# Last stage of a graph kernel: one-hots made on ScalarE, eight of seventeen row tiles split into float32r heads and tails

## What is computed

```python
def _L1_gnn_ref(feat, src_idx, dst_idx, in_deg, W1, b1, W2, b2):
    agg = jax.ops.segment_sum(feat[src_idx], dst_idx, num_segments=num_dst)
    ah = agg / in_deg[:, None]
    return jnp.einsum('nf,of->no', feat[:num_dst], W1) + b1 + jnp.einsum('nf,of->no', ah, W2) + b2

h = jnp.maximum(_layernorm(x, axis=-1), 0.0)
x = x + _L1_gnn_ref(h, src, dst, deg, W1, b1, W2, b2)
```

## Time and profile before

| | before |
|---|---|
| median of 3 runs | 1931.77 us |
| the profiled execution | 1932.3 us |
| its span (first to last instruction) | 1930.5 us |
| the last stage's row tiles on PE (L929), first to last | 1338.8 to 1915.9 us |
| mean granted clock of PE | 0.949 |
| busy over the span: PE, DVE, ACT, POOL | 86%, 69%, 52%, 59% |

### The profile page before, as it was taken

One profiled execution on the slowest core, in us unless ns is written; L12 is line 12 of the kernel. 1 busy time (PEld: TensorE's weight loads), 2 busy tenths in 40 slices (PEclk: granted clock), 3 DMA queues, 4 the chain that ended last, 5 costly groups with the idle time before them and its releaser, 6 DMA issues.

```text
span 1930.5 us, 24219 instructions
## 1 busy us (share of the span) xinstructions
PE 1666.8 (86%) x5735; PEld 963.8 (50%) x5735; DVE 1336.3 (69%) x2587; ACT 1001.1 (52%) x3779; POOL 1141.1 (59%) x1323
## 2 busy tenths in 40 slices
PE   3799863688988889898888897895999999999998
PEld 1344331466666666666666666342444444444443
DVE  8768994888888989898988885465444444444441
ACT  4453313499999999999999997241000000000000
POOL 2000001878787878888787880013777777777773
PEclk9899876799999989999999999997999999999999
DMA  8122104665657565665657562945777777777774
GB/s 188 52 69 71 63 28 145 192 168 143 192 150 190 160 184 170 168 186 163 191 149 197 145 179 61 222 109 153 210 217 212 219 218 219 216 214 211 215 213 140
DMA packets 133201, 318.07 MB, mean 165 GB/s; under 512 B 41908, under 2 KB 42158, under 8 KB 133044
## 3 DMA queue, kind: packets, MB, share of 16 engines
q0 software_dynamic: 70240, 229.93, 41.8%
q1 hardware_dynamic: 62804, 86.44, 16.2%
HBM read 280.43 MB, written 35.86 MB: 164 GB/s over the span
## 4 chain that ended last, share of the span: by engine, by line
PE 51%; DVE 20%; issue 15%; POOL 7%; DMA 4%; ACT 2%; DVEq 1%; SPq 0%; POOLq 0%; ACTq 0%
PE wide L769 14%; PE sums L929 12%; PE sums L832 12%; PE wide L860 9%; POOL arena L504 7%; DVE nodes L1338 2%; DVE arena L1083 2%; DVE arena L1082 2%; DMA h2tab<-node 2%; DVE nodes L1284 1%; DVE nodes L1329 1%; DVE node L1225 1%; PE wide L782 1%; PE wide L787 1%; ACT arena L582 1%
## 5 line engine op out<-in xcount | busy, mean ns | idle before, releaser
L636 ACT ACTIVATE nodes<-arena,nodes 128x64 f32<-128x64 f32 x2840 | 682.7, 332 | 1.2 <-PE sums L832 1.2
L504 POOL DMA_INDIRECT arena<-ktab,idx x425 | 421.5, 992 | 188.1 <-issue 142.2
L504 POOL DMA_INDIRECT arena<-h2tab,idx x425 | 445.7, 1049 | 135.8 <-issue 134.9
L832 PE MATMUL sums<-nodes,oh 128*125 128x260 f32 x1768 | 466.7, 407 | 47.0 <-DVE nodes L1284 47.0
L769 PE MATMUL wide<-w_sb,node 128*125 128x512 f32 x1000 | 465.6, 610 | 20.7 <-ACT node L567 12.3
L832 PEld LDWEIGHTS sums<-nodes,oh 128*125 128x125 f32 x1768 | 342.0, 198 | 123.3 <-DVE nodes L1284 58.4
L929 PE MATMUL sums<-arena,oh 128*125 128x512 f32 x850 | 375.9, 600 | 6.9 <-DMA arena<-h2tab,idx 6.5
L716 ACT ACTIVATE node<-wide 128x500 f32<-128x500 f32 x51 | 27.3, 585 | 570.9 <-PE wide L915 570.8
L860 PE MATMUL wide<-q_win,node 125*128 125x512 bf16 x1275 | 310.3, 381 | 3.0 <-issue 3.0
L769 PEld LDWEIGHTS wide<-w_sb,node 128*125 128x125 f32 x1000 | 187.0, 193 | 230.8 <-issue 201.8
L1329 DVE TENSOR_TENSOR nodes<-wide,arena 128x1024 f32<-128x1024 f32 (+1 forms) x225 | 258.6, 1159 | 12.4 <-PE wide L860 11.8
(11 more groups left out here) (202 smaller groups left out, 1165.9 us busy)
## 6 DMA issues: line engine op xcount, KB each, us to landing
node<-node_tab SPq DMA_DIRECT2D x27, 531.2 KB
q_win<-qtab SPq DMA_DIRECT2D x26, 336.0 KB
arena<-ktab,idx POOLq DMA_INDIRECT x425, 5.1
arena<-h2tab,idx POOLq DMA_INDIRECT x425, 3.9
h2tab<-node POOLq DMA_DIRECT2D x25, 250.0 KB, 2.7
node<-h2tab SPq DMA_DIRECT2D x26, 224.0 KB
qtab<-q_win SPq DMA_DIRECT2D x17, 336.0 KB
nodes<-x SPq DMA_DIRECT2D x5, 1120.0 KB
```

Of the source, the lines that this page charges most:

```text
L504: gp.indirect_dma_start(rows[:, b, t, :], None, tab, bass.IndirectOffsetOnAxis(ap=idx[:, b, t:t + 1], axis=0)).then_inc(s["rows_in"][b][PA ...
L636: last = act.activation(msgs[:, t, h // HH, h % HH * DH:(h % HH + 1) * DH], rows[:, 1 - b, t, h * DH:(h + 1) * DH], ACT.Copy, scale=den_in ...
L832: last = pe.matmul(halves[:, u, :], oh[:, 1 - b, t, :], rhs[side][:, t, u, :], start=t == 0, stop=t == CT - 1)
```

## The change

ACT makes the one-hots: `late_hot` squares (iota - loc) in 17 activations and then turns 1 - square through a Relu of 2125 elements into 0 or 1. The first two chunks' one-hots are made in the stage ahead, after the norms of windows 4 and 8 (`HOT_AT`); the one-hots of chunk g+2 are made in `fin` of chunk g. DVE still sums them over the tiles.

Tiles 3 to 6 and 7 to 10 (`HEADED`) are no longer multiplied as float32. ACT copies the four rows of a group to `heads`, a float32r tile (`make_heads`, an activation of 2048 elements), then copies each of the four to PSUM (`copied`, two buffers in turn); DVE subtracts head from row and writes the rest over the row in float32r (`make_tails`); PE multiplies head and tail with the same one-hots. `tail_made` tells PE that a tail is there and ACT that a buffer is free. The other nine tiles stay as they were. The rows lie in `late_rows`, in the place of `arena`. On DVE the output's additions now come ahead of the sum of the one-hots, and the tails stand in two places.

```diff
@@ block.scalar
+            def late_hot(g, b, done=None):
+                act.wait_ge(ag["decode"], g * 3 + 3)
+                if done is not None:
+                    act.wait_ge(ag["acc_ready"], done)
+                for t in range(CT):
+                    last = act.activation(late_oh[:, b, t, :], iota[:, 0:WIN], ACT.Square, bias=loc[:, b, t + 1:t + 2], scale=-1.0)
+                last.then_inc(ag["oh_ready"], 1)
+                act.wait_ge(ag["oh_ready"], g * 2 + 1)
+                hot = late_oh[:, b, :, :].rearrange("p t n -> p (t n)")
+                act.activation(hot, hot.bitcast(F32), ACT.Relu, bias=ones[:, 0:1], scale=-1.0).then_inc(ag["oh_ready"], 1)
+            def h2_and_hot(t, b, i):
+                h2(t, b, i)
+                if t in HOT_AT:
+                    late_hot(HOT_AT[t], HOT_AT[t])
-            ahead(act, NW, 2, h2_turned, h2)
+            ahead(act, NW, 2, h2_turned, h2_and_hot)
...
+            def make_heads(n, g, b, i):
+                t0, k, part = HEADED[n]
+                act.wait_ge(ag["rows_in"][b][part], (i + 1) * PARTS[part][1] * 16)
+                act.wait_ge(ag["rows_free"][part], g + 2)
+                act.activation(heads[:, n * 4:n * 4 + k, :], late_rows[:, b, t0:t0 + k, :].bitcast(F32), ACT.Copy)
+                for t in range(t0, t0 + k):
+                    m = g * HEADS + HEAD_AT[t]
+                    if not isinstance(m, int) or m >= 2:
+                        act.wait_ge(tail_made, m - 1)
+                    act.activation(copied[HEAD_AT[t] % 2], late_rows[:, b, t, :].bitcast(F32), ACT.Copy).then_inc(head_made, 1)
...
             def fin(g, b, i):
                 fin_turned(1, g * 2 + 2, ag["out_free"])
                 fin_turned(0, g * 2 + 3, s5["row_free"])
+                given(act, within(g + 1, count1), lambda: make_heads(0, g + 1, 1 - b, i + b))
+                given(act, within(g + 2, count1), lambda: late_hot(g + 2, b, g + 1))
+                given(act, within(g + 1, count1), lambda: make_heads(1, g + 1, 1 - b, i + b))
@@ block.tensor, agg
-                        last = pe.matmul(aggp, oh[:, b, t, :], rows[:, b, t, :], start=t == 0, stop=t == CT - 1)
+                        if t in HEAD_AT:
+                            pe.wait_ge(tail_made, g * HEADS + HEAD_AT[t] + 1)
+                            pe.matmul(aggp, late_oh[:, b, t, :], heads[:, HEAD_AT[t], :], start=False, stop=False)
+                            last = pe.matmul(aggp, late_oh[:, b, t, :], late_rows[:, b, t, :], start=False, stop=False)
+                        else:
+                            last = pe.matmul(aggp, late_oh[:, b, t, :].bitcast(F32), late_rows[:, b, t, :].bitcast(F32), start=t == 0, stop=t == CT - 1)
@@ block.vector
             def sum_hot(g, b):
-                one_hot(ag, g, b)
-                dve.wait_ge(ag["oh_ready"], g + 1)
-                dve.tensor_reduce(oh_sum[:, b, :], oh[:, b, :, :].rearrange("p t n -> p n t"), AX.X, ALU.add).then_inc(ag["kept"], 1)
+                dve.wait_ge(ag["oh_ready"], g * 2 + 2)
+                dve.tensor_reduce(oh_sum[:, b, :], late_oh[:, b, :, :].bitcast(F32).rearrange("p t n -> p n t"), AX.X, ALU.add).then_inc(ag["kept"], 1)
...
+            def make_tails(n, g, b):
+                t0, k, _ = HEADED[n]
+                for t in range(t0, t0 + k):
+                    dve.wait_ge(head_made, g * HEADS + HEAD_AT[t] + 1)
+                    dve.tensor_tensor(late_rows[:, b, t, :], copied[HEAD_AT[t] % 2], heads[:, HEAD_AT[t], :].bitcast(F32), ALU.subtract).then_inc(tail_made, 1)
...
                 dve.sem_inc(ag["out_ready"], 1)
                 st.end()
-                def next_hot():
-                    decode(ag, g + 2, b, i + 1)
-                    sum_hot(g + 2, b)
-                given(dve, within(g + 2, count1), next_hot)
+                given(dve, within(g + 2, count1), lambda: decode(ag, g + 2, b, i + 1))
+                given(dve, within(g + 1, count1), lambda: make_tails(0, g + 1, 1 - b))
...
                 dve.tensor_tensor(nout[:, b, 0, :], nout[:, b, 1, :], x_sb[:, bass.ds(w, 1), :].rearrange("p a d -> p (a d)"), ALU.add).then_inc(s5["out_ready"], 1)
+                given(dve, within(g + 2, count1), lambda: sum_hot(g + 2, b))
+                given(dve, within(g + 1, count1), lambda: make_tails(1, g + 1, 1 - b))
```

More of the change, by code:

```diff
@@ L64, in build @@
         chunk_tab = [dram(f"chunk_tab{j}", [GTAB, 2]) for j in range(2)]
-        arena = sb("arena", [128, 2 * CT * D])
+        with ExitStack() as under_rows:
+            arena = under_rows.enter_context(nc.sbuf_tensor("arena", [128, 2 * CT * D], F32))
+        late_rows = sb("late_rows", [128, 2, CT, D], F32R)
         rows = arena[:, 0:2 * CT * D].rearrange("p (b t d) -> p b t d", b=2, t=CT)
@@ L94, in build @@
             ones_row = under_oh.enter_context(nc.sbuf_tensor("ones_row", [BR, 128], F32R))
-        oh = sb("oh", [128, 2, CT, WIN])
+        with ExitStack() as under_late_oh:
+            oh = under_late_oh.enter_context(nc.sbuf_tensor("oh", [128, 2, CT, WIN], F32))
+        late_oh = sb("late_oh", [128, 2, CT, WIN], F32R)
         junk = sb("junk", [128, 2, HALF])
@@ L112, in build @@
         oh_sum = junk[:, 0, 0:2 * WIN].rearrange("p (b n) -> p b n", b=2)
-        q_win = sb("q_win", [WIN, 2, SPLIT, D], BF16)
+        HEADED = [(3, 4, 1), (7, 4, 2)]
+        HEADS = sum(k for _, k, _ in HEADED)
+        HEAD_AT = {t0 + k: n * 4 + k for n, (t0, tiles, _) in enumerate(HEADED) for k in range(tiles)}
+        with ExitStack() as under_heads:
+            q_win = under_heads.enter_context(nc.sbuf_tensor("q_win", [WIN, 2, SPLIT, D], BF16))
+            minus = under_heads.enter_context(nc.sbuf_tensor("minus", [WIN, WIN], BF16))
+        heads = sb("heads", [128, HEADS, D], F32R)
         q_parts = q_win
@@ L176, in build @@
         aggp = sums[0:WIN, 0:D]
+        copied = [wide[k][:, D:2 * D] for k in range(2)]
         degp = tiny[0:WIN, 0:1]
@@ L184, in build @@
         XT = NW // XG
+        HOT_AT = {4: 0, 8: 1}
         COUNTED = 20
@@ L497, in _, with gather @@
             gp.sem_inc(consts, 1)
-            def gather(s, tab, g, b, first=0, end=CT):
+            def gather(s, tab, into, g, b, first=0, end=CT):
                 hold(gp, "pool", s["idx_ready"], g + 1)
@@ L503, in gather @@
                         hold(gp, "pool", s["rows_free"][PART[t]], g + 1)
-                    gp.indirect_dma_start(rows[:, b, t, :], None, tab,
+                    gp.indirect_dma_start(into[:, b, t, :], None, tab,
                                           bass.IndirectOffsetOnAxis(ap=idx[:, b, t:t + 1], axis=0)).then_inc(s["rows_in"][b][PART[t]], 16)
@@ L519, in _ @@
             count = chunk_count(gp, 0)
-            gather(at, ktab, 0, 0)
+            gather(at, ktab, rows, 0, 0)
             def one_hot(g, b):
@@ L531, in attend @@
             def attend(g, b, i):
-                given(gp, within(g + 1, count), lambda: gather(at, ktab, g + 1, 1 - b, 0, PARTS[2][0]))
+                given(gp, within(g + 1, count), lambda: gather(at, ktab, rows, g + 1, 1 - b, 0, PARTS[2][0]))
                 one_hot(g, b)
-                given(gp, within(g + 1, count), lambda: gather(at, ktab, g + 1, 1 - b, PARTS[2][0], CT))
+                given(gp, within(g + 1, count), lambda: gather(at, ktab, rows, g + 1, 1 - b, PARTS[2][0], CT))
             chunks(gp, count, attend)
@@ L548, in _ @@
             count1 = chunk_count(gp, 1)
-            chunks(gp, count1, lambda g, b, i: gather(ag, h2tab, g, b))
+            chunks(gp, count1, lambda g, b, i: gather(ag, h2tab, late_rows[:, :, :, :].bitcast(F32), g, b))
         @block.scalar
@@ L718, in _ @@
             fin_turned(0, 1, s5["row_free"])
+            def make_heads(n, g, b, i):
[8 more added lines that the diff above has]
+                    act.activation(copied[HEAD_AT[t] % 2], late_rows[:, b, t, :].bitcast(F32), ACT.Copy).then_inc(head_made, 1)
+            for n in range(len(HEADED)):
+                make_heads(n, 0, 0, 0)
             def fin(g, b, i):
@@ L1433, in _ @@
             then(dve.tensor_tensor(last_bias[0], last_bias[0], last_bias[1], ALU.add))
+            def make_tails(n, g, b):
[3 more added lines that the diff above has]
+                    dve.tensor_tensor(late_rows[:, b, t, :], copied[HEAD_AT[t] % 2], heads[:, HEAD_AT[t], :].bitcast(F32), ALU.subtract).then_inc(tail_made, 1)
+            for n in range(len(HEADED)):
+                make_tails(n, 0, 0)
             def agg(g, b, i):
```

2 lines of the change are left out of this document (1 added, 1 removed).

## The result

The changed kernel takes **2115.05 us** (median of 4 runs, 2111.34 to 2120.53) where the kernel before takes 1932.03 (4 runs, 1930.68 to 1933.87): a ratio of 1.0949, 95% interval 1.0920 to 1.0978. The profiled execution took 2111.34 us, its span is 2109.5, against 1932.3 and 1930.5 before.

A forecast was written before the change was run, and what follows sets the result against it. PE and POOL were both taken as near 23.4 us a chunk. Loop 30.05 + clock 2.2 = 32.25 us; 1932.3 + 203 (23 transitions) + 4 (stage ahead) = 2139 us, 8-in-10 range 2075 to 2190.

The forecast's parts named there:

- the likeliest case: Whole kernel: the forecast of 2139 us, given 55%, with its own range 2110 to 2170 us, periods of 31 to 33.5.
- the loop: Last stage, each chunk: waits in series through PE, ACT and DVE set a period of 30.05 us before the clock's price.
- Float32r at 0.42 us: Headed tiles on PE: each float32r matmul taken as 0.42 us, 0.84 a tile, no gain against 0.86; lower end 0.21.
- The clock at +2.2 us: Last stage, after PE's idle stretch: clock at 0.50 adds 2.2 us a chunk, bounds 0 and +4.7.
- The case without a price of the clock: Last stage: the loop as summed, but PE's clock stays up or its half rate is hidden; 2089 us, 20%.
- The period of before at 23.42: Last stage of the kernel before: 23.42 us from product to product, PE and POOL both near that.
- POOL's stall: Last stage, one gather a chunk beside DVE's one-hots: 1.6 to 2.1 us longer, gone once the comparison leaves DVE.
- the six other terms: Loop, per chunk: product and transposes 4.15, ACT's copies 1.07, heads 1.91, PSUM copies 2.66, one-hots 7.20, sum 4.21 us.
- The last transition, unchanged: Last stage's final transition, without one-hots and sum: PE's own chain of about 23 us sets it; change 0, bounds -2 and +1.
- The stage ahead at +4: Stage before the last: two one-hot groups of 7.2 us on ACT, partly hidden, add 4 us, from 0 to 2 x 4.7.
- The faster rival: Last stage: one-hots and sum run in idle time, loop 18.6 us, POOL's 21.25 decides; 1880 us, 4%.
- No gather over 1 us: Profile after, POOL's gathers: none longer than 1 us would show the stall gone.

The follow-up runs named there:

- the exchange of two calls on each of two engines: Changed kernel, with part 2's tails ahead of the one-hots' sum on DVE and part 2's heads and copies ahead of the one-hots on ACT: 1962.79 us.
- the busy PE: Changed kernel plus 19 matmuls a chunk into unused PSUM columns ahead of tile 7's wait: 2086.15 us, ratio 1.0786.
- the one-hots alone: Changed kernel without heads and tails, all row tiles multiplied as float32, one-hots still on ACT: 1941.29 us, ratio 1.0042 when run again.
- the heads alone: Changed kernel without ACT's one-hots; DVE makes them just ahead of their sum, heads and tails stay: 2040.27 us, ratio 1.0549 when run again.

## Why the prediction was right, and where its terms were off

The forecast was 2139 us, the time 2115.05, 24 us below it and inside the likeliest case's own range (2110 to 2170). The mechanism stands as put: the loop sets the period, PE idles ahead of tile 7 (8.30 us, 7.4 put), the clock is 0.50 there, and POOL waits, though not for freed buffers as put but for the index that DVE decodes behind PE's last tile. This is shown by the exchange of two calls on each of two engines (-152 us) and by the busy PE (-1.64 us a chunk). The mis-sized terms and misread details:

- **Float32r at 0.42 us**: it is 0.23 at the full clock and 0.43 at the half. The lower bound, 0.21, was the nearer; why the bias matmul, with 33 rows, stood for 0.42 at a clock of 1.00 was not tried. A split tile is 0.46 us instead of 0.86. The Trainium skill (FP8 and Floating Point Precision, TensorE Precision Notes) has four passes for true FP32, and states no number for the reduced form. The float32 matmul, two records of 0.43, took 3.7 times the 0.23 of the float32r one, which agrees with it if the reduced form is one pass.
- **The clock at +2.2 us**: 1.64. The stretch and the levels were right, but halving the clock costs less on a matmul of 0.23 us than on one of 0.42. The case without a price of the clock (2089 us) falls: with the clock held up the period is 29.08, and the changed kernel's is 30.72. The mean clock of the stage, put near 0.7, is 0.84: it is at 0.50 for only 10.2 us of each 30.72.
- **The period of before at 23.42**: I took one transition, which holds a wait for rows that most don't have. It is 23.13 in most, 23.19 on average. And not "both PE and POOL": PE's work sets it, as the one-hots alone showed. POOL's stall, put at 1.6 to 2.1 us, is no fixed amount of work: the gather ends 0.8 us after the comparison, whenever it began.
- **The loop at 30.05** was 29.08 at full clock, 1.0 less: 0.6 from ACT's and DVE's terms, each some 0.1 too long (in the rows above an instruction's record starts some 0.1 before the one ahead of it ends), 0.4 from the headed tiles and those behind them (29.08 less the six other terms, 20.61, is 8.47, against 2.75 + 0.94 + 5.16). With the clock 32.25 against 30.72, so 23 x (30.70 - 23.19) = 173 us in place of 203. That is 30 us of the miss.
- **The last transition, unchanged**: it became 2.9 us shorter. I set it by PE's chain of 23 us. With split tiles at 0.46 that chain is 23.13 - 8 x 0.40 = 19.9 by this estimate, and the loop without one-hots and sum, 21.1 by my terms, is then the longer: 20.2.
- **The stage ahead at +4**: +8.9, nearly the upper bound of 9.4. I took ACT's waits for DVE as room for the groups, but there was none where they stand: the first group delayed the copy of the transposes of window 7 right behind it, and PE waited 8.2 us for it, with the clock at its lower level afterwards.
- **The faster rival** was right about its condition: with the 11.2 us of one-hots and sum off the loop the kernel takes 1888 us, POOL-bound, against 1880 put. Two things in it were wrong. Its loop of 18.6 us left out the heads and copies of part 2, which the sum for the last transition counts (21.1; measured 20.2). And it needs the cheap float32r matmul: at the 0.42 us of the sum PE's own 23 us would have stayed the bound, as in the one-hots alone, where POOL's relief by itself gave nothing.
- **"No gather over 1 us"**: the stall did not go wholly. One gather a chunk still takes 1.4 us in the changed kernel, beside the output's second addition, which also reads two SBUF tiles. It cost nothing, since POOL waited 9.3 us a chunk.

The sum of these is -30 (loop) -3 (last transition) +5 (stage ahead) = -28 on the profiled execution (2111.34 against 2139).

## What to carry to other kernels

Where an engine gets new work that other engines wait for, write down the ring of waits per iteration and put everything in it that is queued ahead of the awaited instruction, needed now or not. Work for later iterations belongs behind the work that the others wait for, on each engine of the ring: here one exchange of two calls on each of two engines was worth 152 us. Only with the ring below the next bound does the relief of the old bound (PE, then POOL) show.

## What the runs showed of the chip that I had not expected

- A float32r matmul of 128x125 by 512 columns starts every 0.23 us at full clock and every 0.43 at half clock; two float32 records of the same take 0.86 (by the eight of the earlier trace rows).
- An idle PE of 8.3 us in every 30.72 had the clock at 0.50 for some 10.2 us of them. Over half of that lay in the idle stretch itself, and the whole cost only 1.64 us.
- A gather that begins beside DVE's comparison, or beside the output's second addition, ends 0.82 us after that instruction does. In the kernel before, the comparison of the earlier trace rows ends at 1504.55 us and the gather at 1505.37; in the next chunk it is 1527.98 (first row below) and 1528.79 (the gather of 3.07 us in the earlier trace rows). So the gather's length, 1.98, 2.51 or 3.07 us, tells only how early in the comparison it began. The difference is 0.81 to 0.82 us in all 22 such gathers of the kernel before and all 23 of the heads alone (from 1370 us on), and in the 21 of the changed kernel beside the addition of 0.69 us:

```profile
1525.60 2.38 DVE L1232 TENSOR_TENSOR oh<-iota,loc 128x2125 f32<-128x2125 f32 x1 [0.18 <-DVE loc L1223]
```

```profile
1625.26 0.69 DVE L1515 TENSOR_TENSOR node<-node,nodes 125x512 f32<-125x512 f32 x1 [0.24 <-DVE node L1512]
...
1625.35 1.43 POOL L516 DMA_INDIRECT late_rows<-h2tab,idx  x1 [0.30 <-issue]
```

- One chip ran the kernel before in 2213 us instead of 1932. There the loop of the changed kernel (with one-hots 0 and 1 behind the stage ahead) kept its 30.72 us, while its last stage started at 1475 us instead of 1360; the cause stays open.
